# Attention scores in two pairs of banks, one exponential for each pair; maxima in two banks, a ring of 10 tiles

## The reference, cut to what matters

```python
HD = 16; HKV = 1
q = (x @ wq_w.T + wq_b).reshape(b, t, H, HD)
k = (x @ wk_w.T + wk_b).reshape(b, t, HKV, HD)
v = (x @ wv_w.T + wv_b).reshape(b, t, HKV, HD)
scores = jnp.einsum('bqhd,bkd->bhqk', q, k1) / jnp.sqrt(jnp.float32(HD))
scores = jnp.where(causal, scores, -jnp.inf)
weights = jax.nn.softmax(scores, axis=-1)
attn = jnp.einsum('bhqk,bkd->bqhd', weights, v1)
return attn.reshape(b, t, H * HD) @ wo_w.T + wo_b
```

## Time and profile before

| | us |
|---|---|
| median of 3 timed runs | 1447.14 (1446.95 to 1448.77) |
| the profiled execution's own time | 1452.08 |
| its span | 1450.3 |
| TensorE matmuls busy | 1274.3 (88%) |
| VectorE busy | 744.3 (51%) |
| ScalarE busy | 431.1 (30%) |
| GpSimd busy | 151.3 (10%) |

### The profile page before, as it was taken

How to read it: one execution, slowest core, us unless ns; L and a number is a source line. 1 busy time by engine, 2 the same in 40 slices (tenths; PEclk the granted TensorE clock), 3 DMA queues, 4 the chain that set the end, 5 groups by cost and what they waited for, 6 DMA issues and landing times. The chain is left out here.

```text
span 1450.3 us, 14475 instructions
## 1 busy us (share of the span) xinstructions
PE 1274.3 (88%) x5250; PEld 831.9 (57%) x5250; DVE 744.3 (51%) x1297; ACT 431.1 (30%) x717; POOL 151.3 (10%) x208
## 2 busy tenths in 40 slices
PE   7999998799799989973656788989999999799998
PEld 4787665344578778762434243444454443488876
DVE  5222323484776545414565564877776642433264
ACT  2122212120311224201222112146666666322141
POOL 0000000000394000001111013001101114000000
PEclk9999999899899999965665799989999999899999
DMA  7110000730355620003000000000000000111000
GB/s 311 44 43 0 0 0 18 308 145 1 131 196 195 219 85 1 0 31 128 0 0 0 0 22 23 0 1 2 1 2 3 2 3 1 44 66 70 17 22 37
DMA packets 18681, 78.82 MB, mean 54 GB/s; under 512 B 3330, under 2 KB 4226, under 8 KB 16452
## 3 DMA queue, kind: packets, MB, share of 16 engines
q1 hardware_dynamic: 18628, 78.13, 14.7%
HBM read 75.76 MB, written 2.10 MB: 54 GB/s over the span
## 5 line engine op out<-in xcount | busy, mean ns | idle before, releaser
L373 PE MATMUL psum<-L_ffn_x,L_ffn_w_up 128*128 128x512 f32 x1152 | 264.4, 391 | 3.2 <-DVE L_ffn_hidden L502 3.2
L373 PEld LDWEIGHTS psum<-L_ffn_x,L_ffn_w_up 128*128 128x128 f32 x1152 | 217.0, 189 | 50.2 <-DVE L_ffn_hidden L502 5.1
L1818 DVE TENSOR_REDUCE mqa_top<-psum 128x1 f32<-128x512 f32 (+3 forms) x304 | 186.0, 656 | 57.4 <-PE psum L1644 37.7
L1737 ACT ACTIVATE mqa_prob<-psum 128x512 f32<-128x512 f32 x288 | 159.8, 601 | 85.7 <-PE psum L1662 84.5
L390 PE MATMUL psum<-L_ffn_wd,L_ffn_part_h 128*128 128x512 f32 x600 | 142.6, 399 | 7.0 <-DVE L_ffn_wd L298 7.0
L1662 PE MATMUL psum<-mqa_stack,mqa_keys 100*128 100x512 f32 x288 | 132.7, 476 | 4.7 <-DMA mqa_stack<-mqa_rows 3.4
L390 PEld LDWEIGHTS psum<-L_ffn_wd,L_ffn_part_h 128*128 128x128 f32 x600 | 115.0, 193 | 31.9 <-DVE L_ffn_part_h L289 7.8
L1633 PE MATMUL psum<-mqa_keys,mqa_stack 96*128 96x512 f32 (+1 forms) x256 | 107.4, 439 | 2.3 <-DVE mqa_top L1818 1.0
L373 PE MATMUL psum<-L_attn_x,L_attn_w_up 128*128 128x512 f32 x456 | 105.4, 393 | 3.9 <-DVE L_attn_hidden L502 3.9
L373 PEld LDWEIGHTS psum<-L_attn_x,L_attn_w_up 128*128 128x128 f32 x456 | 86.7, 190 | 22.5 <-issue 4.3
L1662 PEld LDWEIGHTS psum<-mqa_stack,mqa_keys 100*128 100x128 f32 x288 | 55.3, 196 | 72.0 <-ACT mqa_prob L1737 62.6
(11 more groups left out here) (245 smaller groups left out, 1663.4 us busy)
## 6 DMA issues: line engine op xcount, KB each, us to landing
L_ffn_stage<-in_L_w SPq DMA_DIRECT2D x25, 768.0 KB, 6.3
L_ffn_z_int<-in_L_z SPq DMA_DIRECT2D x14, 768.0 KB, 4.5
L_ffn_s_all<-in_L_s SPq DMA_DIRECT2D x14, 768.0 KB, 6.2
lora_wo<-in_L_wo SPq DMA_DIRECT2D x8, 1024.0 KB, 8.8
L_attn_stage<-in_L_w SPq DMA_DIRECT2D x10, 512.0 KB, 3.6
L_attn_w_down<-in_L_down SPq DMA_DIRECT2D x1, 2560.0 KB, 24.4
x_feat<-in_x_feat SPq DMA_DIRECT2D x2, 1024.0 KB, 7.3
x_tok<-in_x_tok SPq DMA_DIRECT2D x1, 2048.0 KB, 18.9
```

The source lines that it names most:

```text
L373: ins = nc.tensor.matmul(bank[half][:, :], w_up[:, slot, w_part, at:at + P], x[:, x_part, k, half * HALF:(half + 1) * HALF], start=k == 0 ...
L1737: nc.scalar.activation(prob[:, n % PROBS, :], score_bank[n % 3], ACT.Exp, scale=SCALE)\
L1818: nc.vector.tensor_reduce(top[:, i % 2, lo // HALF, heads[0]:heads[-1] + 1], max_bank[n % 3][:, 0:len(heads) * width] .rearrange("p (h k) ...
```

## The change

Scores use four banks (0 to 3) in two pairs. ScalarE does nothing at even scores and takes one exponential of 1024 columns, two banks side by side, at odd ones; all counters of exponentials now count pairs. Only even scores wait for a pair of banks. The maxima have two banks (4 and 5) where they had three. The values move to bank 7 and the queries' projection to banks 0 and 1. The ring of exponentiated tiles has 10 tiles, an even number, where it had 11.

```diff
--- before.py
+++ after.py
@@ -51,7 +51,7 @@
         self.ffn_base["loaded"] = [0, 0]
         self.tails = self.ln_count = 0
         psum = ctx.enter_context(nc.psum_tensor("psum", [P, 8, 512], F32))
-        self.bank = [psum[:, i, :] for i in range(8)]
+        self.psum, self.bank = psum, [psum[:, i, :] for i in range(8)]
 
     def sb(self, name, shape, dt, ctx=None):
         return (ctx or self.ctx).enter_context(self.nc.sbuf_tensor(name, shape, dt))
@@ -1324,7 +1324,7 @@
 
 
 HEADS, HD = 32, 16
-PROBS = 11
+PROBS = 10
 PAIRS = HEADS // 2
 SPLIT = 3 * 2 * HD
 SHIFTED = SPLIT + 4
@@ -1490,7 +1490,7 @@
         o_sb = sb("o_sb", [P, 2, HALF])
         inv = sb("inv", [P, 4, 2, 2])
         attn, a_feat = sb("attn", [P, 2, DIM]), sb("a_feat", [P, 2, KC, P])
-        max_bank, score_bank, value_bank = [c.bank[0], c.bank[1], c.bank[7]], [c.bank[2], c.bank[3], c.bank[5]], c.bank[4]
+        score_bank, max_bank, value_bank = c.bank[0:4], c.bank[4:6], c.bank[7]
         turn_bank = c.bank[6]
 
         w_loaded, wo_loaded, const = weights.w_loaded, weights.wo_loaded, sem("const")
@@ -1500,7 +1500,7 @@
         spread_built, head_rows_built = sem("spread_built"), sem("head_rows_built")
         spread_ready, spread_by_act, spread_by_dve = sem("spread_ready"), sem("spread_by_act"), sem("spread_by_dve")
         key_rows, bo_added, hidden, pool_step = sem("key_rows"), sem("bo_added"), sem("hidden"), sem("pool_step")
-        SPREAD_BANKS, QUERY_BANKS = c.bank[2:4], c.bank[4:6]
+        SPREAD_BANKS, QUERY_BANKS = c.bank[2:4], c.bank[0:2]
         hidden_use, n_diag = {}, 0
         for e in plan:
             if e[0] == "score" and e[4] == order[e[1]]:
@@ -1560,7 +1560,7 @@
                     qt = order[i] if kind not in EARLY else None
                     if kind == "score" and event[4] == qt:
                         n = event[2]
-                        pool.wait_ge(exp_ready, n + 1)
+                        pool.wait_ge(exp_ready, n // 2 + 1)
                         tile = prob[:, n % PROBS, :].rearrange("p (j q) -> p j q", j=4)
                         nc.gpsimd.affine_select(out=tile, in_=tile, compare_op=ALU.is_ge, fill=0.0, base=0,
                                                 pattern=[[0, 4], [1, P]], channel_multiplier=-1).then_inc(hidden, 1)
@@ -1618,8 +1618,8 @@
                         ins.then_inc(spread_ready, 1)
                     elif kind == "max":
                         _, _, n, heads, lo, width = event
-                        if n >= 3:
-                            pe.wait_ge(max_taken, n - 2)
+                        if n >= 2:
+                            pe.wait_ge(max_taken, n - 1)
                         if n == 0:
                             pe.wait_ge(spread_by_act, 8)
                             pe.wait_ge(spread_by_dve, 8)
@@ -1628,7 +1628,7 @@
                             pe.wait_ge(const, 2)
                             pe.wait_ge(key_rows, 4)
                         masked = lo + width == (qt + 1) * P
-                        out = max_bank[n % 3]
+                        out = max_bank[n % 2]
                         if len(heads) == 1:
                             ins = nc.tensor.matmul(out[:, 0:width], stack[0:SPLIT, heads[0] // 2, cols(qt)],
                                                    keys[0:SPLIT, heads[0] % 2, lo:lo + width],
@@ -1656,10 +1656,10 @@
                         if n == 0:
                             pe.wait_ge(spread_by_act, 16)
                             pe.wait_ge(spread_by_dve, 16)
-                        if n >= 3:
-                            pe.wait_ge(exp_ready, n - 2)
+                        if n >= 4 and n % 2 == 0:
+                            pe.wait_ge(exp_ready, n // 2 - 1)
                         g, head = divmod(u, 2)
-                        ins = nc.tensor.matmul(score_bank[n % 3], keys[0:SHIFTED, head, cols(kt)],
+                        ins = nc.tensor.matmul(score_bank[n % 4], keys[0:SHIFTED, head, cols(kt)],
                                                stack[0:SHIFTED, 4 * g:4 * g + 4, cols(qt)],
                                                start=True, stop=True)
                         ins.then_inc(score_ready, 1)
@@ -1671,7 +1671,7 @@
                         if kt == qt:
                             pe.wait_ge(hidden, hidden_use[n])
                         else:
-                            pe.wait_ge(exp_ready, n + 1)
+                            pe.wait_ge(exp_ready, n // 2 + 1)
                         nc.tensor.matmul(value_bank[row:row + 32, :], v[:, kt, :], prob[:, n % PROBS, :],
                                          start=kt == 0, stop=final).then_inc(value_done, 1)
                     elif kind == "heads":
@@ -1731,11 +1731,13 @@
                                        SPREAD_BANKS[0][0:SPLIT, :]).then_inc(spread_by_act, 1)
                     elif kind == "score":
                         n = event[2]
-                        act.wait_ge(score_ready, n + 1)
-                        if n >= PROBS:
-                            act.wait_ge(value_done, n - PROBS + 1)
-                        nc.scalar.activation(prob[:, n % PROBS, :], score_bank[n % 3], ACT.Exp, scale=SCALE)\
-                            .then_inc(exp_ready, 1)
+                        if n % 2:
+                            act.wait_ge(score_ready, n + 1)
+                            if n >= PROBS:
+                                act.wait_ge(value_done, n - PROBS + 1)
+                            at, two = (n - 1) % PROBS, (n - 1) % 4
+                            nc.scalar.activation(prob[:, at:at + 2, :], c.psum[:, two:two + 2, :], ACT.Exp,
+                                                 scale=SCALE).then_inc(exp_ready, 1)
                     elif kind == "value" and event[4] and event[3] % 4 == 3:
                         _, _, n, u, _, _ = event
                         four = 2 * i + u // 4
@@ -1816,7 +1818,7 @@
                         _, _, n, heads, lo, width = event
                         dve.wait_ge(max_ready, n + 1)
                         nc.vector.tensor_reduce(top[:, i % 2, lo // HALF, heads[0]:heads[-1] + 1],
-                                                max_bank[n % 3][:, 0:len(heads) * width]
+                                                max_bank[n % 2][:, 0:len(heads) * width]
                                                 .rearrange("p (h k) -> p h k", h=len(heads)), AX.X, ALU.max)\
                             .then_inc(max_taken, 1)
                     elif kind == "shift":
```

## The result

The changed kernel takes 1482.98 us (median of 4 runs, 1479.26 to 1486.6) against 1447.18; the ratio is 1.0243, with a 95% interval of 1.0216 to 1.0271. The forecast was 1479.6, in a range of 1461 to 1495. The span of the profiled execution went from 1450.3 to 1484.9 us, 34.6 more.

What follows compares the result with a forecast made beforehand. TensorE, without slack in the attention, was taken as the bound, with bank return times deciding. 15.3 + 5 + 6.5 + 5.7 = 32.5 us more took the profiled 1452.08 to 1484.6, and the timed median 1447.14 to 1479.6; range 1461 to 1495.

Steps and rivals of the forecast that it cites:

- The maxima: Attention: losing the third maxima bank costs 15.3 us in rounds with maxima and 5 us before the first score.
- the pair and the diagonal: Attention: the wide exponential costs 6.5 us in the last rounds, later masks of diagonal tiles cost 5.7 us.
- Maxima in two banks: Rounds with maxima: each max load waits for the reduction two before, not three; 15.3 us, bounds 6 and 24.
- The recurrence of 0.68, 0.05, 0.50 and 0.04: One maxima bank's turn: reduction, delay to the waiting load, load to matmul's end, delay to reduction; 1.27 us.
- Maxima before the first score: 64 maxima alone and between the queries: 0.635 us each with two banks, not 0.60; 5 us, bounds 0 and 9.
- rival 2: Last rounds: more gaps drop TensorE's clock to half speed, adding 20 to 28 us, about 1502; chance 0.05.
- One exponential for two scores: Rounds without maxima: last score waits for a 1.03 us pair, +0.43 in 15 rounds; 6.5 us, bounds 0 and 9.
- The diagonal: Diagonal rounds: GpSimd gets two masks late, values wait; 0.5 in 7 rounds, 0.25 in 9; 5.7 us, bounds 1 and 10.
- Moved at no cost: Query banks, value bank and ring of 10 tiles: moved or resized without any new wait, no cost.
- The first (maxima hide): Attention: bank waits overlap with scores, leaving the wide exponential's 12 us and a few, 1459 to 1463; chance 0.08.
- The third (ScalarE's queue decides): Exponentials set the pace, so 144 pairs give back 8.6 us, 1438.5; chance 0.02.
- The fourth (a pair of 1.19 us): Pair no cheaper than two singles: +0.16 in last and diagonal rounds, about 1485; chance 0.83 together with the forecast.

Runs made afterwards that it cites:

- e1: Kernel before with two banks for the maxima instead of three, nothing else changed: 1473.96 us, ratio 1.0188.
- e2: Changed kernel with one 512-column exponential per score again, keeping four score banks and two maxima banks: 1470.16 us, ratio 1.0167.
- e3: Changed kernel with the values of four scores due five scores after the last of them instead of four: 1464.45 us, ratio 1.0134.
- e4: Changed kernel with a third bank for the 64 maxima before the first score, two afterwards: 1480.26 us, ratio 1.0247.
- e5: Changed kernel with single 512-column exponentials for the 64 diagonal tiles, the other 224 in pairs: 1475.44 us, ratio 1.0198.
- e6: Kernel before, with scores using all six banks from score 228 on: 1445.31 us, ratio 0.9983, not resolved in the time.
- e7: Kernel before with the values due six scores after the last of their four instead of four: 1440.39 us, ratio 0.9962.
- e10: Kernel before with six score banks from score 228 on and values due five scores later instead of four: 1438.45 us, ratio 0.9952.
- e8: Kernel before with six score banks from score 228 on and values due six scores later instead of four: 1442.32 us, ratio 0.9947.
- e9: As e8, but six banks from score 234 and a second maximum at every eighth, not fifth, score of the first query tile: 1441.26 us, ratio 0.9943.

## Why the prediction was right

The forecast was 32.5 us more, and 35.8 were measured, 35.3 of them inside the attention of the traces. The mechanism held part by part, but the closeness of the sum is partly luck. The maxima were put at 20.3 us and cost 23.9 (e1); the pair and the diagonal were put at 12.2 and cost 9.4 (changed kernel against e1, without the end); the end, 1.9, was not in the sum.

*Maxima in two banks* was the bulk, as forecast. The recurrence of 0.68, 0.05, 0.50 and 0.04 gave rounds of 3.53 us and got them to a hundredth. With five it gave 4.20 to a measured 4.23. Masked rounds of 512 columns grew by 0.14 to 0.16 where 0.16 was forecast, between scores 155 and 167. Those with five masked maxima of 384 columns grew by 0.40 to 0.44 where 0.35 was worked out. Scores 0 to 227 took 17.6 us more in e1, against 15.3, and 19.1 in the changed kernel, against 15.3 and 2.2 for the diagonal. The largest part of what is missing is at the start: scores 3 to 15 took 3.4 more where three rounds of 0.66 make 2.0. The granted clock over these scores was 0.75 in the changed kernel and 0.85 before; in e2, at 0.79, they took 2.8 more. I had no term for that.

*Maxima before the first score* were forecast at 5 and cost 6.4, inside the bounds. What was missing is the clock. I had figured 0.635 for each at the old matmul time. They took 0.79 in the changed kernel, as the granted clock fell from 0.79 to 0.63, so most of the stretch was at the 1.2 GHz level. e2 has the same two banks at 0.81 between 902 and 920; its first reductions run 0.65 apart, and there this stage costs 4.1 and not 6.4. So about 2 us are the clock, and rival 2 was right in kind but named the wrong place: in the last rounds the clock stayed at 1.00.

```profile
902.00:920.00 18.00, 15.69 (x28) 7.27 (x27) 12.23 (x19) 0.05 (x1) 0.00 (x0) 0.62 0.00 0
...
902.00:920.00 18.00, 16.04 (x35) 7.39 (x35) 14.85 (x23) 0.69 (x1) 0.00 (x0) 0.81 0.00 0
```

The first line is of the changed kernel, the second of e2.

*One exponential for two scores.* 1025 ns for 1030. The undisturbed last round went to 3.03 for 3.04, and e2 and e3 show the wait from both sides.

*The diagonal.* The extra in a diagonal round without maxima is 0.58 where 0.60 was worked out. Both terms together were put at 6.5 + 3.5 for the last rounds and came to 7.8. The over-estimate is in the count of rounds. Of the 14 rounds from score 231 on, 13 are longer by 0.41 to 0.44 for the bank (15 were counted), and only 4, not 7, carry the 0.58 of the mask on top: 13 x 0.43 + 4 x 0.58 = 7.9. In two other diagonal ones, from score 271 and 279, transposes or a projection stand in between, and the seventh lies behind score 287. The nine diagonal rounds with maxima took 2.3 us more than in e1, where 2.2 was forecast, but 0.8 came back in the rounds between.

*Slips that changed nothing.* The pair of banks that the round's last score waits for holds the scores three and four back, not two and three; the round's first is one of them either way. The unmasked maxima behind the first query tile are 52, not 51. The upper end of the range was said to be where the upper bounds of the maxima and the diagonal meet; they add up to 1492.6, and to 1496.6 with the maxima ahead of the first score.

*Moved at no cost* holds. The ring of ten was not tested alone; neither the trace after nor e2, which keeps it, shows a wait of ScalarE for the values.

*Rivals.* The first (maxima hide) fell with e1. The third (ScalarE's queue decides) fell with e2: taking the pair out makes the kernel faster, and the 15 us less of ScalarE's busy time on the page (431.1 to 416.3) bought nothing. The fourth (a pair of 1.19 us) fell with the 1.025 of the trace. The fixed 0.3 us per activation of the Trainium skill, "ScalarE: Activation LUTs", "Rules for kernel authors", would have made 1.15; the trace has 1.025, so a fixed part near 0.17. That row of the Trainium skill is for an activation whose bias is a pointer operand, and this kernel's exponential is given none, so the prediction used it outside its condition.

The end, 1.9 us longer, was not forecast. The granted clock there (the last 22 to 26 us) was 0.92 before, 0.86 in the changed kernel, 0.77 in e4, whose end is the longest at 25.4, and 0.92 in e1, whose end is 21.7. e2, e5 and e6, whose last scores have single exponentials, have 23.0 to 23.4 at 0.86. So about 1.5 of the 1.9 go with the clock; likely, but not tested. The other 0.4 are the pair again: ScalarE copies the features of the last but one tile (L1757) only behind the wide exponential, and the transposes behind that copy wait 1.45 us, where they waited 1.02.

What stays open: the values' delay gives 3.9 us between scores 0 and 227 in e7 (4.9 less the group of values that moved out), and the wait at L1649, 4.1 less, accounts for it. In e3 it gives 5.2 by the same count, and this wait fell only from 2.1 to 0.8; where the rest goes was not settled. What makes the granted clock of the first maxima 0.62 or 0.81 with the same two banks is open too.

## What to carry to other kernels

Count buffers by the round trip of one of them and by how the uses bunch, not by the busy share of the engine that empties them. VectorE was idle for a third of the attention. A bank took 1.27 us to turn, 0.635 for each max with two, and a round of 3.07 us has only one max per 0.77 us; on the average two banks would do. But all four stand ahead of the values, where TensorE loads one every 0.47 us. There the third bank held the surplus until the values, behind which VectorE caught up. Without it TensorE waited, and as it had no slack, the wait stayed. Whether two banks are enough with one of the four maxima behind the values was not tested.

Before making an instruction wider, ask which of its halves comes first, and who waits for that one. Here the same pair cost 8 to 9 us in the last rounds in one place and about 2 one score further on (60.5 against 51.4 with single ones, e2; 51.6 in e3 against 49.7, e10). When a wait has been removed, look for the next late thing in the same round: more banks alone gave 1.3 us there and later values alone about 1.2, both together about 3.9, the moved transposes left out.

## What the runs showed of the hardware

An exponential from PSUM takes 597 ns for 512 columns and 1025 for 1024 across two banks; two wide ones in a row take 1.94 to 1.95, so 0.92 each, against 0.49 for a single. Reading across the border of a bank costs nothing that shows: 597 ns and the 0.43 of 512 more columns in the casts make 1.03 as well.

The same stage can get either clock, and a spare bank hides which. Over the first 18 us of the first maxima the granted clock was 0.81 in the kernel before, e4, e6, e7 and e10 and 0.72 in e8 and e9, and with their three banks the stage took 55.9 to 56.1 us in all seven. With two banks it was 0.62 in the changed kernel, e1, e3 and e5, for 62.2 or 62.3 us, and 0.81 in e2, for 60.0. At the lower level a max matmul behind a wait lasts 0.80 us, at the higher 0.50, and each bank's turn is longer by that. So a bank that is just missing can cost more than its recurrence at full speed says.

The spread of a kernel's own times goes with the clock as well: of 24 runs of the kernel before, the fastest, 1444.28 us, had a mean granted clock of 0.922 and the slowest, 1452.05 us, 0.915.
